# AdaLN two-layer kernel on one core: identity products ahead of each attention pass, and score matmuls issued twice

## The reference, cut to what matters

```python
def step(carry, i):                      # 3 iterations
    qp = qcur @ lq_w.T + lq_b
    sq = _ln(qp, lnc_w) * tscale
    sk = _ln(kp, lnd_w)
    scores = jnp.einsum('bhqd,bhkd->bhqk', sq, sk) * inv_sqrt_e
    scores = jnp.where(in_win[None, None, None, :], scores, -jnp.inf)
    probs = jax.nn.softmax(scores, axis=-1)
    out = jnp.einsum('bhqk,bhkd->bhqd', probs, vp)
    iter_out = jnp.where(in_win[None, None, :, None], out, 0.0)
    diff = jnp.mean(jnp.abs(iter_out - prev))
    ...                                  # window, temperature, next queries
    qcur_n = jnp.where(upd, qcur + iter_out, qcur)
```

## Time and profile before

| | |
|---|---|
| runs | 526.44, 529.2 and 526.31 us, median 526.44 |
| profiled execution | 531.3 us, span of its instructions 529.5 us |
| PE busy / DVE busy / ACT busy / POOL busy | 330.6 / 312.7 / 176.5 / 155.2 us |
| mean granted clock of PE | 0.723 of 2.4 GHz |
| the three iterations in the span | about 32 to 75, 84 to 146 and 168 to 218 us |

### The profile page before, as it was taken

The page is one execution under the profiler, slowest core; times in us unless marked ns, Lnnn a source line. Parts: engine busy times, 40 slices in busy tenths (PEclk is TensorE's granted clock), DMA queues, the critical chain, the costliest instruction groups (busy, mean ns, idle before and its releaser), DMA issues.

```text
span 529.5 us, 7928 instructions
## 1 busy us (share of the span) xinstructions
PE 330.6 (62%) x2189; PEld 240.8 (45%) x2190; DVE 312.7 (59%) x912; ACT 176.5 (33%) x340; POOL 155.2 (29%) x240
## 2 busy tenths in 40 slices
PE   2947896799001889777999994370561710398780
PEld 1732254334001332567999984360351600387680
DVE  6898959854008995384556551137588881075570
ACT  1034641174000157043455451035701540053340
POOL 9223826406750000012000046704000027233351
PEclk9865575559555558878999997575587555599996
DMA  2799000001110000002122222111900002323210
GB/s 67 194 373 358 3 1 1 0 2 36 55 56 4 0 0 1 12 20 71 55 74 59 64 80 64 55 41 39 351 3 1 1 17 93 100 67 73 71 52 0
DMA packets 36217, 34.57 MB, mean 65 GB/s; under 512 B 6259, under 2 KB 26949, under 8 KB 36192
## 3 DMA queue, kind: packets, MB, share of 16 engines
q1 hardware_dynamic: 32432, 26.83, 16.4%
q0 software_dynamic: 3712, 7.44, 4.7%
q10 hardware_dynamic: 48, 0.00, 0.0%
HBM read 19.92 MB, written 14.79 MB: 66 GB/s over the span
## 4 chain that ended last, share of the span: by engine, by line
PE 40%; DVE 25%; another core or an unknown queue 11%; issue 7%; ACT 5%; POOL 3%; DVEq 1%; DMA 1%; SPq 0%; ACTq 0%; POOLq 0%
PE ps L1096 11%; PE ps L1107 10%; PE ps L934 4%; DVE mx L1585 4%; PE ps L909 3%; PE ps L929 3%; POOL rows L503 3%; PE ps L885 2%; DVE stats L1232 2%; ACT wide L655 1%; PE ps L1086 1%; PE ps L956 1%; DVE w_now L1716 1%; DVE wide L1808 1%
## 5 line engine op out<-in xcount | busy, mean ns | idle before, releaser
L503 POOL DMA_INDIRECT rows<-token_rows,posu x48 | 48.7, 1014 | 183.1 <-DVE posu L1484 104.2
L1096 PE MATMUL ps<-xsT,w_now 128*128 128x128 f32 x552 | 82.7, 298 | 26.1 <-issue 18.3
L1724 DVE TENSOR_TENSOR hb<-ps,b_in 128x512 f32<-128x512 f32 x69 | 47.6, 690 | 80.4 <-PE ps L1096 52.3
L1096 PEld LDWEIGHTS ps<-xsT,w_now 128*128 128x128 f32 x552 | 73.6, 208 | 31.9 <-issue 21.8
L1107 PE MATMUL ps<-w_out,hg 128*128 x552 | 78.7, 290 | 7.7 <-issue 3.6
L1107 PEld LDWEIGHTS ps<-w_out,hg 128*128 128x128 f32 x552 | 71.9, 204 | 9.9 <-issue 9.9
L738 ACT ACTIVATE hg<-hb 128x512 f32<-128x512 f32 x69 | 43.4, 630 | 52.3 <-DVE hb L1724 46.6
L1585 DVE TENSOR_REDUCE mx<-ps 128x2 f32<-128x512 f32 (+2 forms) x48 | 44.4, 948 | 4.7 <-PE ps L909 4.3
L909 PE MATMUL ps<-feat,qs 64*128 64x281 bf16 (+2 forms) x128 | 33.3, 432 | 13.5 <-DVE mx L1585 9.9
L516 POOL DMA_INDIRECT y<-back,posu x16 | 15.6, 972 | 88.7 <-DMA back<-ys 81.3
L643 ACT COPY qs<-ps 128x768 bf16<-128x768 bf16 (+1 forms) x21 | 15.3, 727 | 77.8 <-PE ps L885 77.8
(11 more groups left out here) (346 smaller groups left out, 530.2 us busy)
## 6 DMA issues: line engine op xcount, KB each, us to landing
rows<-zeros SPq DMA_DIRECT2D x22, 256.0 KB, 6.9
xs<-rows SPq DMA_DIRECT2D x69, 64.0 KB
back<-ys SPq DMA_DIRECT2D x46, 64.0 KB
w_in<-in_L_ffn_w_fc SPq DMA_DIRECT2D x1, 2048.0 KB, 15.2
w_in<-in_L_ffn_W SPq DMA_DIRECT2D x1, 2048.0 KB, 8.9
rest<-rows SPq DMA_DIRECT2D x23, 65.0 KB
token_rows<-in_L_attn_x SPq DMA_DIRECT2D x1, 832.0 KB, 8.8
wmod<-in_L_wmod SPq DMA_DIRECT2D x2, 384.0 KB, 4.3
```

Of the source, the lines that this page charges most:

```text
L503: pool.indirect_dma_start(ROWS[l], bass.IndirectOffsetOnAxis(ap=posu[:, k, j:j + 1], axis=0), token_rows[:, j, 0:WIDTH[l]], None).then_inc ...
L1096: mm = pe.matmul(ps[:, c % RING, n * P:(n + 1) * P], w_now[:, c % 2, n * P:(n + 1) * P], xsT[:, c % 2, :], start=True, stop=True)
L1724: v.tensor_tensor(hb[:, c % 2, :].rearrange("p (b t) -> p b t", b=NB), ps[:, c % RING, :].rearrange("p (b t) -> p b t", b=NB), b_in[:, l, ...
```

## The change

`scores` goes through its `nj` query blocks twice. The second round writes the same products to the same PSUM places, and the signal to DVE is given by the last matmul of the second round. `scores_t` is untouched. Ahead of the wait for `q_stack` PE issues 30, 24 and 66 products of the bf16 identity with itself in iterations 0, 1 and 2, into a part of PSUM bank 4 that nothing reads before the scores overwrite it. They wait for nothing.

```diff
                         pe.wait_ge(sem("max_free"), H0 + h + 1)
-                        for j in range(nj):
+                        for j in (*range(nj), *range(nj)):
                             mm = pe.matmul(ps[:, 3 * b + j, 0:nw], half(qs, h)[:, j * P:(j + 1) * P], half(ks, h)[:, 0:nw], start=True, stop=True)
                         mm.then_inc(sem("s_ready"), 1)
...
+                for _ in range((30, 24, 66)[it]):
+                    pe.matmul(ps[:, 4, 0:P], identb[:], identb[:], start=True, stop=True)
                 pe.wait_ge(sem("q_stack"), it + 1)
                 turn(0)
```

## The result

The changed kernel takes **544.0 us** (median of 4 runs, 540.04 to 549.56) where the kernel before takes 527.82 in the same session (4 runs, 526.31 to 534.32). The ratio is 1.029, 95% interval 1.016 to 1.042: slower, but whether by 2% the interval leaves open. The profiled execution took 540.88 us with a span of 539.1, against the 529.5 us span of before.

The account below looks back on a forecast made before the run. The bound was taken to be a chain of waits with two of four heads' score matmuls on it, not DVE's busy share. 526.4 + 13.9 - 0.3 = 540 us; own range 535 to 547, for 8 in 10 down to 530.

Parts of the forecast that it names:

- streams on the chain at a low clock: First passes: two of four heads' score matmuls lie on each round's chain of waits, at 1.2 GHz; seven streams an iteration.
- The rounds: First passes, four heads each: 4.60 to 6.00 us in iteration 1, 4.91 to 6.45 in iteration 2.
- the sum: Whole kernel: doubled streams of 3.0, 4.9 and 5.4 us plus head 0 make +13.9; identity products -0.3.
- only streams next to the turn count: First-pass rounds: the last head before the turn and the first behind it cannot hide; two streams a whole round.
- The clock stayed low: All three first passes: PE's clock taken as 1.2 GHz despite the denser score work.
- gaps and transposes: First passes: 64-row work with a tenth of transposes and gaps still in it, so the clock was taken as low.
- The identity products: Before each iteration's first turn: 30, 24, 66 hidden by DVE's work, costing 0, 0 to 0.1 and 0 us.
- head 0's doubled scores: First head of each first pass, partly hidden: nothing in iteration 0, 0.2 us in iteration 1, 0.4 in iteration 2.
- Nothing swallows it: Between stages: delay passes on whole; the scatter begins later by iterations 0 and 1's loss, DVE resumes behind it as before.
- if that wait shrinks or grows: DVE's wait behind POOL's scatter: its end and the scatter's start both some 8 us later; otherwise the sum is off.

Follow-up runs that it names:

- the first trace: Profiled execution of the changed kernel in the first session, beside the kernel before: 540.88 us, span 539.1.
- the second run of the changed kernel: The changed kernel unaltered, rerun on another chip against the kernel before: 492.21 us, ratio 1.036 (1.028 to 1.044).
- the late scatter: The kernel before, with POOL's scatter of the far rows held until DVE has finished iteration 2's queries: 475.08 us, ratio 0.993.
- the first pair: The changed kernel and the kernel before, measured in the first session: 544.0 against 527.82 us, ratio 1.029.

## Why the prediction was right, and where its steps were off

The main mechanism, streams on the chain at a low clock, is what the runs show. That the total also came out right owes something to luck, as the parts below say.

*The rounds held.* Forecast 6.00 and 6.45 us in iterations 1 and 2, measured 6.01 and 6.47; iteration 0 went from 3.14 to 3.99 where 3.14 + 2 x 0.43 = 4.00. In iteration 1 one of the rounds grew by only 0.95 us, since it had taken 5.06 before (93.07 to 98.13). From the first maximum to the last, the three first passes grew by 2.99, 4.48 and 5.45 us, 12.9 together; the sum had 13.3 for these streams. The reading that mattered was the chain of the earlier trace rows: the windows of the earlier trace rows showed 5 us of spare time on PE, and little of it could be used. The step that only streams next to the turn count was too neat: the inner heads cost 4.1 us when doubled alone.

*The clock stayed low, for a reason the prediction had half.* The earlier trace rows were read as work on 64 rows against work on 128, and the runs bear that out: doubled 64-row streams left the clock at 1.2 GHz, the same streams on 128 rows took it to 2.4. The prediction also put weight on gaps and transposes. Gaps alone do not explain it: single 128-row streams had the clock up for most of iteration 1's first pass (0.90, PE busy for 10.99 of 16.56 us), and it stayed up across idle stretches of 0.4 to 1.2 us, while a stream without any gap but with half of its time on 64 rows left it at 0.50 in the one execution that was traced. But density does play a part, since in iteration 0 only the doubled 128-row streams raised it. What the turns do to the clock was not tested by itself. The statement of the Trainium skill (TensorE: Matmul & The Clock Gate, part 4) that a transpose does not count as busy time in the same way is not settled by these runs: 24 transposes between 31.9 and 34.6 us left the clock at 0.50 in the kernel before, and with the identity products behind them it was up 0.6 us after the first of these (34.34), which took 2.14 us for all 30.

*The identity products* were put at 0, 0 to 0.1 and 0 us. In the first trace they made DVE wait for 1.96 us in iteration 1 and 0.87 in iteration 2. From the stack to the first maximum iteration 1 took 8.04 us and not 5.00, 3.04 more: the wait, and 1.2 us by which DVE's masks of the keys were slower (3.02 against 1.84 us; why is not shown), less small gains. In iteration 2 the same step took 6.28 us and not 5.53. Where the products were hidden, in the second run of the changed kernel, these steps took 5.28 and 6.04 us, so head 0's doubled scores cost some 0.3 and 0.5 (forecast 0.2 and 0.4). In iteration 1 PE itself was late: the products start at 88.17, behind `turn_out` and the router's matmuls, 0.47 us before the stack is ready, so 2.5 us of products find a gap of 0.5. In the earlier trace rows that gap was 2.72 us. DVE's stack had come 5.1 us later than before and PE's own work some 7.3 (88.17 against 83.60 - 2.72 = 80.88), because the stretch ahead ran at 1.2 GHz all the way; the prediction did not allow for that. On the chip where it could be compared the gap was there and they cost nothing.

*A term that was missing.* In the kernel before, the clock rises late in iteration 0's second part (the 0.59 over 54.20 to 76.00 in the earlier trace rows); in the changed one that stretch is at 0.50. The second part started 2.76 us late (57.02 against 54.26) and ended 5.10 late (80.14 against 75.04): 2.3 us that belong to no term of the sum. It is tempting to put this down to the longer first pass, but the other traces do not bear that out. From the last maximum of iteration 0 to the first of iteration 1 the clock is 0.65 in the trace with doubled scores alone (33.68 us) and 0.50 in one with single scores, that of the late scatter (36.36 us). The clock in this stretch differs between traces either way, and what decides it was not found.

*Where the delay goes.* "Nothing swallows it" failed. The scatter moved by 12.6 us, DVE's end of waiting by 4.85, so 7.8 us were swallowed. The prediction had said that if that wait shrinks or grows the account is wrong, and it is: the wait does not end at a fixed distance from the scatter's start (37.1 us behind its start before, 29.3 after). What it waits for the profile calls "remote", and no run here shows it.

The errors nearly cancel. The streams 12.9 us, the missing clock 2.3, and 3.0 and 0.8 between stack and first maximum in iterations 1 and 2 make 19.0. Less 7.8 of swallowed wait that is 11.2. The start of the experts does come 11.2 us later (234.1 against 222.9), and the span grew by 9.6, with 1.6 given back behind it. Against the 13.6 of the sum that is some 4 too little. The profiled execution (540.88 against 531.3 us of before) is the second fastest of its four; the median, at 544.0, lies 3.1 us above it. Median against median the growth is 16.2 us where the sum had 13.6. That the forecast of 540 lies so near is in part luck: costs of 5 to 6 us that it did not have were met by a wait that swallowed 7.8.

## What to carry to other kernels

Filling idle slots of TensorE with more of the same 64-row work did not raise its clock, and where the work stood in a ring of two buffers with VectorE the added streams next to the turn were paid nearly in full: read the chain of one round before calling an engine's idle time spare. Ask how many rows of the array the work uses: with zeros in the unused half of one operand the same count of matmuls ran on 128 rows, the clock was up for most of the time in all passes behind the first, and the kernel became 3.3% faster. Before laying a shift of a few microseconds to a change, look whether the clock in that stretch differs between executions anyway. Before giving filler work a price of nothing, carry the delay of the earlier stages forward to its gap.

## What was not expected of the hardware

- **Rows and the clock.** PE busy for 28.03 of 28.03 us with half of its time on 64 rows: granted clock 0.50 in the execution that was traced. PE busy for 10.99 of 16.56 us on 128 rows: 0.90, though half of the rows of one operand were zeros. The row of the granted clock tells more than the busy share.
- **One kernel, two times.** The kernel before takes 527.8 us in the first pair and 475 to 478 on the chips of the other runs; the first pair's chip is not on record. About half of the difference lies in one place: from the last maximum of iteration 1 to the first of iteration 2 it takes 66.68 us, and 39.85 in the run with doubled scores on another chip. There DVE (33.10 us), ACT (15.97 us) and PE stand idle for long, which the profile puts down to "remote" or "issue", beside POOL's 26 indirect transfers. The rest lies behind the attention, with such waits of up to 11.26 us beside later indirect transfers. The same 26 transfers in the same 1.27 us steps did not stop these engines on the other chips. What differs was not found.
- **ACT as a multiplier costs more than a copy.** A copy of 128x768 took 0.81 us (four of them, 2.91 together), the product with a column of ones and zeros a median of 0.92. Eight in place of four nearly fitted into ACT's slack of iteration 0: the first maximum came at 43.2 us, and at 42.4 in the kernel before (42.1 to 42.9 in the runs without the second copy of the keys).
